# A small language-model tower: weights prepared on four engines beside their loads, first ids loaded early, statistics between the attentions moved into the first one's loop

## The reference, cut to what matters

```python
h = tok_ref(six id arrays, six tables, W, b, gamma, beta)      # concat of embeddings @ ternary(W).T + b, layer norm
h = h + L0_attn(layernorm(h))    # linear attention: elu(q)+1, elu(k)+1, 8 heads of 8;
                                 #   D_inv = 1.0 / maximum(q . k_sum, 1e-6)
h = h + L0_ffn(layernorm(h))     # gelu(x @ W1 + b1); top-1 of 8 experts, weighted by its probability
h = h + L1_attn(layernorm(h))    # softmax attention over 1024 tokens, 8 heads of 64, out projection
h = h + L1_ffn(layernorm(h))     # 4 heads of 16 with 4 query sets, causal softmax; gating; two small
                                 #   linear layers with masks; layer norms; softmax gate per head
return h
```

## Time and profile before

| | us |
|---|---|
| median of 3 runs | 5478.77 (5478.61 to 5479.2) |
| the profiled execution, its own time | 5484.4 |
| its span, first to last instruction | 5482.7 |
| loads, constants, weights | 0 to 136.6 |
| layer 0 | 136.6 to 1023 |
| first attention | 1023 to 3199 |
| statistics | 3199 to 3236 |
| residual | 3236 to 3266 |
| second attention | 3266 to about 5270 |
| rest | to 5482.7 |

### The profile page before, as it was taken

How to read it: one execution, slowest core, us unless ns; L and a number is a source line. 1 busy time by engine, 2 the same in 40 slices (tenths; PEclk the granted TensorE clock), 3 DMA queues, 4 the chain that set the end, 5 groups by cost and what they waited for, 6 DMA issues and landing times. The chain is left out here.

```text
span 5482.7 us, 122251 instructions
## 1 busy us (share of the span) xinstructions
PE 4875.2 (89%) x41817; PEld 2220.9 (41%) x41847; DVE 3828.5 (70%) x7062; ACT 3156.4 (58%) x3362; POOL 2198.4 (40%) x2098
## 2 busy tenths in 40 slices
PE   2687877799999999999999958999999999999965
PEld 1243443333333333333333333444444444444433
DVE  2566666466666666666666647888888888888878
ACT  0222222266666666666666625777777777777754
POOL 1022122332233222332233236556655655565556
PEclk9788788799999999999999968999999999999975
DMA  1311111000000000000000000000000000000001
GB/s 15 91 32 46 31 46 31 1 2 2 1 2 1 2 1 2 1 2 1 2 1 2 1 1 2 2 3 3 2 3 3 3 2 3 3 2 3 2 5 27
DMA packets 43526, 52.90 MB, mean 10 GB/s; under 512 B 33164, under 2 KB 33295, under 8 KB 42896
## 3 DMA queue, kind: packets, MB, share of 16 engines
q1 hardware_dynamic: 39686, 43.82, 3.0%
q10 hardware_dynamic: 3210, 0.90, 0.1%
HBM read 39.70 MB, written 4.19 MB: 8 GB/s over the span
## 5 line engine op out<-in xcount | busy, mean ns | idle before, releaser
L1552 DVE TENSOR_REDUCE a_mp<-psum 128x1 f32<-128x512 f32 x2072 | 1321.7, 685 | 677.1 <-PE psum L1429 672.6
L2188 DVE TENSOR_REDUCE f_mp<-psum 128x1 f32<-128x512 f32 (+2 forms) x2614 | 1343.9, 574 | 234.2 <-PE psum L2036 182.5
L1986 ACT ACTIVATE f_prob<-psum,escale_f 128x1024 f32<-128x1024 f32 x1152 | 1242.7, 1112 | 280.2 <-PE psum L2104 149.1
L1401 ACT ACTIVATE a_prob<-psum,escale 128x1024 f32<-128x1024 f32 x1024 | 1087.9, 1111 | 521.7 <-PE psum L1478 521.5
L1486 PE MATMUL psum<-a_prob,a_v 128*64 128x512 f32 x4104 | 995.7, 606 | 0.0
L2026 PE MATMUL psum<-f_kf,f_qf 64*128 64x512 f16 (+3 forms) x3138 | 677.1, 332 | 51.2 <-DVE f_mp L2188 43.9
L1871 POOL TENSOR_SCALAR f_hi<-f_raw,part 128x512 f16<-128x512 f32 x330 | 516.6, 1566 | 472.6 <-ACT f_raw L1953 472.6
L2117 PE MATMUL psum<-f_prob,f_vh 128*32 128x512 f32 (+3 forms) x6144 | 614.8, 495 | 3.0
L1331 POOL TENSOR_TENSOR a_u<-a_og,a_inv 128x512 f32<-128x512 f32 x129 | 134.5, 1043 | 1149.9 <-DVE a_inv L1567 1149.9
L2096 PE MATMUL psum<-f_qf,f_kf 64*128 64x512 f16 (+3 forms) x3074 | 513.5, 329 | 28.6 <-issue 11.8
L1486 PEld LDWEIGHTS psum<-a_prob,a_v 128*64 128x64 f32 x4104 | 249.2, 136 | 512.0 <-issue 509.0
(11 more groups left out here) (421 smaller groups left out, 7311.7 us busy)
## 6 DMA issues: line engine op xcount, KB each, us to landing
l_idx<-in_itok_BS_dram SPq DMA_DIRECT2D x36, 512.0 KB, 5.6
l_idx<-in_itok_BS_dram SPq DMA_DIRECT2D x54, 256.0 KB, 6.7
l_idx<-in_x_dram SPq DMA_DIRECT2D x18, 256.0 KB, 3.8
a_qh<-a_rowT SPq DMA_DIRECT2D x258, 1.0 KB
out_dram<-h SPq DMA_DIRECT2D x16, 256.0 KB, 2.6
f_qf<-f_rowT SPq DMA_DIRECT2D x130, 4.0 KB, 1.8
wd<-in_L_ffn_Wd_dram ACTq DMA_DIRECT2D x1, 256.0 KB
wd<-in_L_ffn_Wd_dram SPq DMA_DIRECT2D x1, 256.0 KB
```

The lines of the kernel that those rows point to most:

```text
L1401: act.activation(prob[:, part], k.psum[:, pair:pair + 2].rearrange("p b n -> p (b n)"), ACT.Exp, scale=k.escale[:]).then_inc(s.read, 1)
L1552: dve.tensor_reduce(mp[:, tg % 2, t + 4 * r, c:c + 1], bank_of(j + r), X, ALU.max)\
L1986: act.activation(prob[:, u % NPF], k.psum[:, pair:pair + 2], ACT.Exp, scale=k.escale_f[:])\
L2188: ins = dve.tensor_reduce(side[:, at:at + 1], bank_of(j + r)[:, col:col + nk], X, ALU.max)
```

## The change

**Setup.** The three blocks become one, `setup`. The single list of steps is replaced by one list and one semaphore per engine, and each instruction names the results that it needs. All eight PSUM banks are used; transposes that belong together go to one bank and are copied out at once. Copies are spread over VectorE, ScalarE and GpSimd. Loads are in three groups: `urgent` (W, b, the embedding tables), which the table needs, `loads` and `diagonal`.

**Ids.** `idx` gets two sides and a semaphore each; the ids of batches 0 and 1 are loaded within the setup, and each later load is started two batches ahead.

```diff
+def load_ids(k, sp, b, side):
+    for name, c, lo, hi in zip(k.id_names, (0, 0, 1, 2, 3, 3), (0, 64, 0, 0, 0, 64), (64, 128, 128, 128, 64, 128)):
+        sp.dma_start(k.idx[lo:hi, side, c:c + 1], k.ids[name][ds(b, 1), :].partition_broadcast(hi - lo)).then_inc(k.ids_in[side], 16)
...
         @block.sync
         def _(sp):
-            for dst, src in loads[::2]:
+            sp.dma_start(urgent[0][0], urgent[0][1]).then_inc(first, 16)
+            need(sp, "eblk")
+            for dst, src in urgent[1:4]:
+                sp.dma_start(dst, src).then_inc(first, 16)
+            load_ids(k, sp, 0, 0)
+            for dst, src in loads[:len(loads) // 2 - 6]:
                 sp.dma_start(dst, src).then_inc(loaded, 16)
-            sp.wait_ge(cleared, 3)
-            for dst, src in diagonal:
+            load_ids(k, sp, 1, 1)
+            need(sp, "mgate")
+            for dst, src in diagonal[len(diagonal) // 2:]:
                 sp.dma_start(dst, src).then_inc(loaded, 16)
...
+            need(pe, "clear", "eblk")
+            pe.wait_ge(first, n_first)
+            for j in range(4):
+                last = turn(ps[1][0:VR, j * P:(j + 1) * P], k.eblk[:, j])
+            signal(last, "eblk_turn")
...
+            need(pe, "weff_out", "eblkT")
+            for j in range(4):
+                last = mm(ps[2][:, j * C:(j + 1) * C], k.eblkT[:, j], k.weffT[:])
+            signal(last, "table")
+            pe.wait_ge(loaded, n_loads)
+            for n in range(NH):
+                turn(ps[0][0:D, n * C:(n + 1) * C], k.fq[:, n])
...
+            need(pe, "aq_out", "ak_out")
+            for h in range(HEADS):
+                last = mm(ps[7][:, h * C:(h + 1) * C], k.aqT[:, h].rearrange("c a i -> c (a i)"), k.akT[:, h])
+            signal(last, "aqk")
```

**Layer 0, VectorE.** The clamp is joined with the product (the reciprocal of the unclamped sum is bounded by 1e6), and the first tile of a slot stands between the two batches:

```diff
-                            link(dve.tensor_scalar(rs[:, j], ps[3 + 2 * j], 1e-6, None, ALU.max))
-                            link(dve.reciprocal(rs[:, j], rs[:, j]))
+                            link(dve.reciprocal(rs[:, j], ps[3 + 2 * j]))
                             done("num", b + 1)
-                            dve.tensor_tensor(aT[:, j], ps[j], rs[:, j], ALU.mult).then_inc(E["aT"], 1)
+                            dve.scalar_tensor_tensor(aT[:, j], rs[:, j], 1e6, ps[j], ALU.min, ALU.mult).then_inc(E["aT"], 1)
...
+                        if j == 0 and back is not None:
+                            for tile in L_TILES[n][0:1]:
+                                outputs(back, tile)
...
-                        for tile in L_TILES[n]:
+                        for tile in L_TILES[n][0 if front is None else 1:]:
                             outputs(back, tile)
```

```diff
+                def squares(n):
+                    passed(pool, k.seen, s.mean, n + 1)
+                    pool.tensor_tensor(cen[:], k.h[:, ds(n * T, T)], wide(k.mean_f[:, ds(n * T, T)], C), ALU.subtract)\
+                        .then_inc(s.cen, 1)
+                    passed(pool, k.seen, s.cen, n + 1)
+                    pool.tensor_tensor(cen[:], cen[:], cen[:], ALU.mult).then_inc(s.squared, 1)
...
+                        if x % HEADS == 3:
+                            squares(i * 2 + x // HEADS)
...
+                for n, at in ((NB, slice(0, NB * T)), (NB + 1, slice(NB * T, (NB + 1) * T))):
+                    act.wait_ge(s.var, n)
+                    act.activation(k.rstd_f[:, at], k.rstd_f[:, at], ACT.Sqrt, bias=k.eps_ln[:], scale=1.0 / C)\
+                       .then_inc(s.root, 1)
...
+                            if u == 2 and x % HEADS == 2:
+                                means(i * 2 + x // HEADS, i * AROUND + x)
+                            if u == 2 and x % HEADS == 5:
+                                variances(i * 2 + x // HEADS)
+                early = slice(0, NB * T)
+                dve.wait_ge(s.root, 1)
+                dve.reciprocal(k.rstd_f[:, early], k.rstd_f[:, early])
                 inverses(1, NB * HEADS, SS + SR * (NB // 2) + 1)
+                means(NB, NB * HEADS + 2)
...
```

**Second attention, start.** GpSimd only prepares batch 0 and clears `oc` and `og`. VectorE clears `sx`, `vh` and `mp`, and splits x and the first keys and queries:

```diff
+                def first_split(n, tg, kind, e):
+                    dve.wait_ge(s.read, n + 1)
+                    for half in range(2):
...
+                        dve.tensor_scalar(hi[:, r % 2], raw[:, (r // 2) % 2, half], k.part[:, side:side + 1], None, ALU.mult)\
+                           .then_inc(s.hi, 1)
+                        dve.wait_ge(s.hi, at)
...
+                        dve.tensor_tensor(to[:, half * HALF:(half + 1) * HALF], raw[:, (r // 2) % 2, half], hi[:, r % 2],
+                                          ALU.subtract).then_inc(s.laid, 1)
```

More of the change, by code:

```diff
@@ L174, in load_weights @@
     ]
+    diagonal = []
     for n in range(NH):
@@ new lines, in setup, with need, signal @@
+def setup(k, nc, a):
+    ps = k.bank
+    first, loaded, rows_in = k.sem("first"), k.sem("loaded"), k.sem("rows_in")
+    ready = {eng: k.sem("ready_" + eng) for eng in SETUP}
+    where = {name: (eng, n + 1) for eng, names in SETUP.items() for n, name in enumerate(names)}
+    def need(eng, *names):
+        for name in names:
+            by, count = where[name]
+            eng.wait_ge(ready[by], count)
+    def signal(ins, name):
+        ins.then_inc(ready[where[name][0]], 1)
+    urgent, loads, diagonal = weight_loads(k, a)
+    n_first, n_loads = 16 * len(urgent), 16 * (len(loads) + len(diagonal))
@@ new lines, in _ @@
+            need(act, "eblk")
+            for dst, src in urgent[4:]:
+                act.dma_start(dst, src).then_inc(first, 16)
+            for dst, src in loads[len(loads) // 2 - 6:]:
+                act.dma_start(dst, src).then_inc(loaded, 16)
+            need(act, "mgate")
+            for dst, src in diagonal[:len(diagonal) // 2]:
+                act.dma_start(dst, src).then_inc(loaded, 16)
+            need(act, "consts")
+            for x, to in ((0, k.wq2), (1, k.wp2)):
+                for r in range(2):
+                    at = slice(r * C, (r + 1) * C)
+                    copy(("wq", "wp")[x] + str(r), to[at, at], ps[3][at, x * C:(x + 1) * C], "qkv_turn")
@@ new lines, in _ @@
+            copy("wvo", k.wvo[:, :, 0:C], ps[1].rearrange("p (h c) -> p h c", h=HEADS), "avo")
+            need(act, "fall_out")
+            for e in range(2):
+                for i in range(2):
+                    at = 32 * (2 * e + i)
+                    copy(f"wsx{e}{i}", k.wsx[:, :, at:at + D], k.fall[:, i:NH:2, 6])
+            copy("wv", k.wvf[:, 0].rearrange("p (n d) -> p n d", n=NH), k.fall[:, :, 5])
+            copy("wx", k.wvf[:, 1].rearrange("p (n d) -> p n d", n=NH), k.fall[:, :, 6])
@@ new lines, in biggest, with inverse @@
+            def biggest(name, out, in_, axes, needs=()):
+                need(dve, *needs)
+                signal(dve.tensor_reduce(out, in_, axes, ALU.max, apply_absolute_value=True), name)
+            def inverse(name, out, in_, needs=()):
+                need(dve, *needs)
+                signal(dve.reciprocal(out, in_), name)
+            signal(dve.memset(k.eblk[:], 0.0), "eblk")
+            signal(dve.memset(k.fc[:], 0.0), "fc")
+            signal(dve.memset(k.mgate[:], 0.0), "mgate")
@@ L540, in _ @@
-            part_of = (k.fhi, k.flo)
+            copy("fhi", k.fhi[:], k.fnorm[:], ["fnorm_k"])
+            tt("flo", k.flo[:], k.fnorm[:], k.fhi[:], ALU.subtract, ["fhi"])
+            need(dve, "flo", "consts")
             for i in range(2):
@@ L2401, in finish1, with count @@
         stored = k.sem("z_stored")
-        E = {name: k.sem("z_" + name) for name in Z_EVENTS}
+        E, STEP = {}, {}
+        for names in Z_EVENTS:
+            sem = k.sem("z_" + names.replace(" ", "_"))
+            for n, name in enumerate(names.split()):
+                E[name], STEP[name] = sem, (len(names.split()), n + 1)
+        def count(event, batches):
+            each, at = STEP[event]
+            return (batches - 1) * each + at
         def turned_over(ap):
```

782 lines of the change are left out of this document (354 added, 428 removed).

## The result

The changed kernel takes 5361.7 us (median of 4 runs, 5361.2 to 5365.5), the kernel before 5479.0 beside it: ratio 0.9787, 95% interval 0.9775 to 0.9799, so 117 us faster. The forecast was 5327 with 5303 to 5360. The sign and most stages came out; 33 of the 152 us that the sum promised are missing. The profiled execution took 5365.5 us, its span is 5363.8, against 5482.7 before: 118.9 us to account for.

The account below looks back on a forecast made before the run. It took seams as pure latency, layer 0's loop as a chain through engines, the attention as TensorE's. 76.6 + 18.6 + 24 + 1.4 - 8 + 30.2 + 9 = 152 us saved; forecast 5327 us, range 5303 to 5360.

Parts of the forecast that it names:

- the walk: Layer 0's loop, slot 9 stepped through with measured durations: hidden product 3.4 us earlier per turn, 24 us in seven turns.
- the clamp: Layer 0's loop: the clamp instruction goes, 0.69 us twice per turn; also 1.4 us in the front half before the loop.
- a rival of its own: Layer 0's loop: shorter wait at tile 15 keeps TensorE at 2.4 GHz, 2 to 3 us per turn, 5310; chance 0.09.
- The rival by which tiles in between pay nothing: Layer 0's loop: VectorE waits for TensorE in slots 4, 5, 7; the turn keeps 106 us, total 5351; chance 0.14.
- L: Setup: the moment when all loads have landed, taken as 31 us, bounds 27.5 and 38.
- the rival of the ids that hold up the weights: Setup: everything lands at 38 us or later, total 5335 to 5340; chance 0.06 for beyond 38.
- the insertions: First attention: statistics operations placed inside it, a loss of 8 us, bounds 0 to 30.
- the first ids with the front half: Start of layer 0: both id sets already loaded saves 18.6 us, the clamp gone before the loop 1.4.
- the seam of the statistics: End of the first attention: the statistics block is replaced by a 6.5 us tail, saving 30.2 us (28 to 32).
- the second attention's start: Preparation starts at once, clearing beside it on VectorE; first maximum earlier, saving 9 us (6 to 12).
- the semaphores: Last stage: merged semaphores make no wait end later, zero; bounds a gain of 1 and a loss of 5.
- the side estimate of 1.6 us in part 5: Second attention's start: at a full twofold VectorE rate the sum for splitting ten halves would be 1.6 us lower.

Follow-up runs that it names:

- the waits filled: The changed kernel, tiles still between the batches, with four idle TensorE products in slot 4's wait and two in slot 7's: 5329.1 us.
- slot 9's order alone: The changed kernel with an output tile taken between the two batches in slot 9 only, in slots 3 to 8 all behind both: 5314.7 us.
- all three waits filled: Kernel with only slot 9's tile between and sums behind u = 1, plus idle products: six in slot 9, two in slot 2, four in slot 4: 5319.6 us.

## Why the prediction was wrong, step by step

- **Failed: "TensorE has tiles queued in front of that work, so only 0.3 us is left beside the clamp's 1.4".** In the walk slot 9's first normalisation comes 0.3 us later in the turn than before, the clamp included; it comes 1.94 later (first part 75.32 to 77.26 us). The clamp gave 2.2 there (75.28 to 73.04), the tiles in between took 4.2 (73.04 to 77.26). With the waits filled only 1.1 of these are left (74.11), so the rest is TensorE's clock: the tiles lengthen waits behind which it runs at 1.2 GHz. With what follows in slot 9, the order in slots 3 to 8 costs 6.3 us per turn, 44 in seven.
- **Failed too: the walk ends where the hidden product begins.** Up to there it is right: 9.9 us behind slot 9's first normalisation instead of 13.7, the wait at tile 15 at 6.14. But it took this shift, 3.7 in the walk and 3.8 measured, for the gain of the whole second part, which fell by 1.5 (29.54 to 28.05), since the hidden product then took 3.7 us for 1.99. The prediction gave the clock a rival of its own, but looked for it at tile 15, where it is worth nothing, and for a gain. Of the 3.9 us per turn that are missing (a loss of 0.45 for a gain of 3.4) 1.6 are in the first part and 2.2 in the second. That slot 9's order alone is worth 3.25, close to the 3.4, is partly luck: 0.50 of it is in the first part, and 2.75 is what the clock left of 3.8. Why the clock is back before the hidden product in one order and not in the other, no run isolates.
- **The rival by which tiles in between pay nothing** has about the right turn (105.3 on average, 106 forecast) for the wrong reason: one slot pays and six take it back. By the prediction's own sign, a turn not below 105 us, this part is wrong.
- **Mis-sized: the clamp,** 2.6 us per turn for the 1.4 of its two instructions. The turn of 106.3 us that was walked is one of six that average 104.86. The bounds of the step, a gain of 6 and a loss of 2, did hold the result (a loss of 0.45).
- **Mis-sized: L,** 38.2 for 31, just beyond the upper bound of 38, so the rival of the ids that hold up the weights came true; in the other runs with these loads it is 34.3 to 37.4, and this profile is the latest of them. The sum of shares was near (31.5 us for 30.4), though not its terms: apart, the weights take 10.2 and the ids 16.3. What was missing is that the engines reach only 0.93 of the stretch and that landing is seen 3.4 us late. The chain behind L took 25.7 us for 29, so the block ended at 63.9 for 60: 3.9 us short.
- **Mis-sized: the insertions,** a loss of 16.7 us for 8: 0.50 us in head 2 and 0.28 in head 5 for 0.4 and 0.1: 12.5 us, and 0.13 us in head 3 of every second batch. 3.2 us more lie at the loop's ends (18.2 to 20.5 us for that head in the changed kernel, 18.3 to 20.4 before); with the sums one step earlier they are gone too.
- **Right:** the first ids with the front half (21.1 for 20.0), the seam of the statistics (30.6 for 30.2; its sign, 8 us from the last addition, was wrong, it is 3123.42 to 3128.64, 5.2), the second attention's start (10.1 for 9, first maximum 27.7 us after the residual), the semaphores at nothing. Two small sums are off: 30.2 less 11.5 is 18.7, not 18.6, and the side estimate of 1.6 us in part 5 comes to 1.5 (ten times 0.49 less half of 0.69); neither matters.

Together: 23.2 us missing in layer 0 (24.3 in the turns, less 1.1 that its start gave in excess), 8.7 in the attention, 3.9 in the setup, against some 3 us more elsewhere. The range ends at 5360, and the time is 1.7 us beyond: it did not let the loop, L and the insertions fail together.

## What to carry to other kernels

An instruction slipped between two batches should stand in a wait of its own engine, read from the timeline: the same sum costs 0.5 us behind one read-out and nothing behind the one before it. Take a reordering slot by slot, since one slot can pay what six give away, and keep only those that pay: with slot 9's order alone, the sums at u = 1 and the ids behind the landed weights the kernel takes 5294.8 us, 67 less than the changed one. Where an engine waits a few us several times per turn, judge a reordering by the other engine's busy time for the same work, for that shows what its clock adds.

## What the runs showed of the hardware

- Small delays can cost several times their length through TensorE's clock: of the 4.2 us that the order added to the first part of a turn, 1.1 were left once its waits were filled. Four products after the longer wait took 3.20 us for 1.88, and TensorE was busy 522 us for what it did in 491.
- Idle products in front of a wait's end keep the products right behind it at 2.4 GHz (granted clock 0.95 for 0.81 in slots 4 to 7; tile 15 at 1.98 us for 3.78). That does not hold them there further on: with all three waits filled the hidden product, 3 us of waiting later, took 3.4 to 3.8 us for 1.99 in five of six turns.
- The turns of one loop differ by up to 3.7 us (103.0 to 106.7) and still come back one by one in another program with the same loop; with the changed order five of six lie at 105.74 to 105.82. The state of TensorE's clock at the turn's start seems to be handed from turn to turn; that is argued from the lengths, no run isolates it.
- One program, with six, two and four idle products more in layer 0, paid 2.1 to 3.4 us more than the changed kernel at each of seven loop ends of the second attention, whose code is the same. This stays open.
